# Second attention of a four-layer kernel: the masked sum cut to the masked keys, the open keys read by ScalarE, and a new table of places

## What is computed

```python
x = L0(x, ctx)                 # instance norm, attention over channels, 1x1 convolutions
x = L1(x, ctx, mask1)          # grouped attention, 32 heads on 8 key heads, residual, layer norm
# L2: queries from x, keys and values from ctx and x together (64 + 64 keys)
h    = concatenate([ctx, x], axis=1)
attn = einsum('bkhd,bnhd->bhkn', q(x), k(h)) / 16
full = concatenate([mask2.astype(bool), ones((b, 64), bool)], axis=-1)
attn = softmax(where(full[:, None, None, :], attn, -inf))
x    = mlp(rmsnorm(out(attn @ v(h)) + x)) + x
# L3: layer norm, token shift, five mixes, r k v g and a decay w
s_t  = k_t * v_t + w_t * s_(t-1);  out_t = r_t . (u * k_t * v_t + s_(t-1))
x    = x + (groupnorm(out) * gn_w + gn_b) * g @ Wo.T ; then a channel mix
```

## Time and profile before

| | us |
|---|---|
| median of 3 runs | 2051.25 (2050.09 to 2053.39) |
| the profiled execution | 2052.37 |
| its span, first to last instruction | 2050.3 |
| mean granted TensorE clock, of full | 0.931 |
| busy: TensorE, VectorE, ScalarE, GpSimd | 1742.5, 1383.6, 855.7, 818.8 |
| one group beside a layer 3 | 238.5 |

### The profile page before, as it was taken

The page is one execution under the profiler, slowest core; times in us unless marked ns, Lnnn a source line. Parts: engine busy times, 40 slices in busy tenths (PEclk is TensorE's granted clock), DMA queues, the critical chain, the costliest instruction groups (busy, mean ns, idle before and its releaser), DMA issues.

```text
span 2050.3 us, 36747 instructions
## 1 busy us (share of the span) xinstructions
PE 1742.5 (85%) x13613; PEld 1076.0 (52%) x13613; DVE 1383.6 (67%) x2332; ACT 855.7 (42%) x1687; POOL 818.8 (40%) x895
## 2 busy tenths in 40 slices
PE   3788898898988898898988989888988889888865
PEld 2565555564564645555555645646455555555213
DVE  3653579756886569946787567865788557983383
ACT  1445443444534434454534445344344444343202
POOL 3532147503664136702465036641366114760070
PEclk9999999999999999999989989999999999999757
DMA  6001011110211002110111102110021100210030
GB/s 171 1 1 34 1 22 42 23 43 1 46 25 42 18 1 59 28 26 18 27 38 23 43 1 43 28 43 17 1 59 28 27 17 17 48 23 12 0 83 11
DMA packets 73584, 60.92 MB, mean 30 GB/s; under 512 B 38960, under 2 KB 56512, under 8 KB 73408
## 3 DMA queue, kind: packets, MB, share of 16 engines
q1 hardware_dynamic: 49600, 41.70, 9.6%
q10 hardware_dynamic: 23264, 16.85, 3.0%
q0 software_dynamic: 544, 0.03, 0.0%
HBM read 20.28 MB, written 4.19 MB: 12 GB/s over the span
## 4 chain that ended last, share of the span: by engine, by line
PE 52%; DVE 19%; ACT 11%; issue 9%; POOL 6%; DVEq 0%; ACTq 0%; DMA 0%; POOLq 0%; SPq 0%
PE bank L639 24%; PE bank L974 5%; PE bank L776 5%; PE bank L655 3%; DVE seg_max L1415 3%; PE bank L871 3%; DVE late L1249 3%; DVE soft_ring L1409 3%; PE bank L716 2%; DVE late L1261 2%; POOL late L1537 2%; ACT soft_ring L1111 2%; POOL soft_ring L1575 2%; ACT soft_ring L1121 1%; PE bank L847 1%
## 5 line engine op out<-in xcount | busy, mean ns | idle before, releaser
L1575 POOL TENSOR_TENSOR soft_ring<-soft_ring,seg_max 128x512 f32<-128x512 f32 x256 | 286.0, 1130 | 343.7 <-DVE seg_max L1415 343.1
L1583 POOL TENSOR_SCALAR soft_ring<-soft_ring,rden 128x256 f32<-128x256 f32 x64 | 59.2, 925 | 511.0 <-DVE rden L1374 511.0
L1121 ACT ACTIVATE soft_ring<-soft_ring 128x512 f32<-128x512 f32 x256 | 160.3, 629 | 239.0 <-POOL soft_ring L1575 225.9
L1537 POOL TENSOR_TENSOR late<-late 128x520 f32<-128x520 f32 x128 | 198.2, 1549 | 124.8 <-DMA late<-late 64.8
L1249 DVE TENSOR_TENSOR_SCAN late<-late 128x520 f32<-128x520 f32 x128 | 218.7, 1709 | 15.3 <-DVE early L1430 4.4
L716 PE MATMUL bank<-late,pick 128*128 128x512 f32 x256 | 168.7, 756 | 35.6 <-DVE late L1261 35.1
L1409 DVE SCALAR_TENSOR_TENSOR soft_ring<-bank,mask 128x512 f32<-128x512 f32 x256 | 164.3, 683 | 19.2 <-PE bank L776 8.2
L917 PE MATMUL bank<-ident,soft_ring 128*128 128x128 f32 x1024 | 164.4, 288 | 9.0 <-ACT soft_ring L1121 6.8
L1415 DVE TENSOR_REDUCE seg_max<-soft_ring 128x8 f32<-128x512 f32 (+1 forms) x256 | 166.5, 677 | 6.2 <-DVE early L1472 2.0
L917 PEld LDWEIGHTS bank<-ident,soft_ring 128*128 128x128 f32 x1024 | 117.4, 144 | 95.1 <-issue 66.5
L776 PE MATMUL bank<-early 64*128 64x512 f32 (+1 forms) x512 | 118.5, 564 | 50.3 <-ACTq L1114 47.7
(11 more groups left out here) (240 smaller groups left out, 3337.6 us busy)
## 6 DMA issues: line engine op xcount, KB each, us to landing
late<-late SPq DMA_DIRECT2D x128, 260.0 KB, 3.0
c<-in_ctx ACTq DMA_DIRECT2D x8, 512.0 KB, 4.2
x<-in_x ACTq DMA_DIRECT2D x8, 512.0 KB, 5.3
out_x<-late SPq DMA_DIRECT2D x8, 512.0 KB, 2.9
mask<-in_mask_Bx1xSxS_ff ACTq DMA_DIRECT2D x16, 128.0 KB, 4.5
w<-in_L_xattn_mlp_w ACTq DMA_DIRECT2D x2, 1024.0 KB
mask<-in_mask_BxS_ik SPq DMA_DIRECT2D x8, 256.0 KB, 3.7
wkv<-in_L_xattn_kv_w ACTq DMA_DIRECT2D x1, 512.0 KB
```

The source lines that it names most:

```text
L1121: af(soft[:, u % SOFT, :], soft[:, u % SOFT, :], ACT.Exp).then_inc(sig("exp"), 1)
L1537: tt(aj[:, n % 2, :], kP[:, k, :, :].rearrange("p b t -> p (b t)"), vj[:, n % 3, :], ALU.mult).then_inc(sig("kv_done"), 1)
L1575: tt(s, s, seg_max[:, u % SOFT, 0:segs].unsqueeze(2).broadcast_to([128, segs, 512 // segs]), ALU.subtract).then_inc(sig("sub"), 1)
```

## The change

In the second attention `masked` covers only the first 64 keys of each of the four heads (128 x 256 in place of 128 x 512) and signals `masked2`. A new function on ScalarE, `open_keys`, waits for that signal, reads the other 64 keys of each head from the same bank, scales them and writes them to the same slot, and signals `open2`. It is called for both units of a pair in even iterations, behind `turned`. `largest` waits for both signals, and the bank is given back to TensorE there, by VectorE, and no longer by `masked`. `mask2` loses its half of zeros (and its memset, 128 x 1024, in the setup). The gate of layer 3 is written as two instructions with three operands in place of three (times, times-plus, times). And the tables `PLACES` and `SCAN_PLACES` have other numbers throughout: which step of the main loop a stage of layer 3 stands at, on each engine. The diff, without the counts of the semaphores, the memset and the mask's shapes:

```diff
@@ -509,41 +508,41 @@
 PACE = {"r u k": 2.2, "shift": 2.2, "maa": 2.2, "gate": 2.4, "shift 2": 2.2,
         "mix 4": 1.0, "r": 1.0, "v": 1.0, "decay": 1.0, "td": 1.2}
 PLACES = {
-    "moments": (0, 2, 0, 6),
-    "normalize": (11, 2, 6, 6),
-    "turn": (11, 11, 10, 6),
-    "shift": (11, 26, 15, 6),
-    "maa": (21, 27, 16, 6),
-    "mix 0": (25, 32, 25, 8),
-    "mix 1": (29, 32, 27, 16),
-    "td": (30, 32, 30, 17),
-    "k": (30, 32, 30, 19),
-    "mix 2": (30, 32, 31, 21),
-    "decay": (33, 32, 31, 21),
-    "v": (37, 34, 35, 21),
-    "mix 3": (37, 40, 36, 27),
-    "mix 4": (43, 40, 40, 32),
-    "r": (45, 43, 41, 43),
-    "g": (45, 44, 43, 43),
-    "r u k": (45, 45, 46, 53),
-    "bonus": (50, 52, 55, 55),
-    "center": (123, 123, 123, 127),
-    "variance": (123, 123, 123, 133),
-    "gate": (123, 123, 123, 133),
-    "project": (127, 127, 126, 133),
-    "moments 2": (130, 128, 126, 133),
-    "normalize 2": (130, 129, 132, 133),
-    "turn 2": (132, 130, 133, 133),
-    "shift 2": (133, 130, 133, 133),
-    "ffn k": (134, 133, 133, 133),
-    "ffn r": (134, 133, 133, 133),
-    "ffn v": (134, 133, 134, 133),
+    "moments": (1, 0, 0, 0),
+    "normalize": (1, 1, 1, 4),
+    "turn": (6, 3, 5, 4),
+    "shift": (10, 13, 6, 5),
+    "maa": (11, 21, 8, 5),
+    "mix 0": (25, 25, 24, 5),
+    "mix 1": (28, 27, 26, 5),
+    "td": (28, 28, 27, 5),
+    "k": (30, 30, 29, 18),
+    "mix 2": (33, 30, 33, 26),
+    "decay": (37, 34, 35, 26),
+    "v": (37, 34, 37, 39),
+    "mix 3": (37, 39, 37, 42),
+    "mix 4": (41, 43, 41, 42),
+    "r": (45, 43, 46, 45),
+    "g": (48, 47, 48, 48),
+    "r u k": (50, 66, 49, 48),
+    "bonus": (51, 76, 49, 48),
+    "center": (125, 124, 126, 128),
+    "variance": (127, 126, 126, 128),
+    "gate": (127, 128, 126, 128),
+    "project": (130, 128, 128, 128),
+    "moments 2": (130, 130, 128, 128),
+    "normalize 2": (131, 132, 131, 128),
+    "turn 2": (133, 132, 132, 128),
+    "shift 2": (134, 132, 133, 128),
+    "ffn k": (134, 133, 134, 131),
+    "ffn r": (134, 133, 134, 134),
+    "ffn v": (134, 133, 134, 137),
 }
 SCAN_PLACES = (
-    (50, 52, 64, 56), (50, 61, 65, 64), (61, 62, 68, 64), (69, 68, 69, 65), (70, 75, 70, 66),
-    (72, 81, 70, 66), (80, 85, 85, 70), (82, 100, 85, 82), (86, 100, 89, 94), (92, 107, 98, 102),
-    (103, 111, 105, 105), (103, 112, 107, 105), (110, 112, 107, 106), (110, 112, 107, 106), (111, 112, 109, 117),
-    (111, 112, 112, 117), (121, 123, 117, 123), (121, 123, 120, 123), (123, 123, 122, 126),
+    (62, 76, 57, 52), (63, 77, 64, 58), (67, 77, 67, 63), (67, 77, 68, 64), (70, 81, 68, 64),
+    (72, 81, 70, 70), (82, 81, 84, 71), (83, 86, 85, 84), (87, 89, 86, 86), (88, 89, 97, 94),
+    (94, 92, 100, 102), (107, 112, 106, 102), (109, 112, 107, 107), (111, 112, 109, 110), (115, 112, 112, 116),
+    (120, 113, 119, 128), (123, 113, 119, 128), (125, 117, 119, 128), (125, 118, 122, 128),
 )
 due = {}
 for stage in STAGES:
...
             if now:
                 sp.wait_ge(sig("max"), past("max"))
-            sp.dma_start(mask2[:, :, 0:L].bitcast(I32), mask2_in[now].unsqueeze(0).broadcast_to([128, NB, L])).then_inc(sig("mask2_in"), 16)
+            sp.dma_start(mask2[:, :, :].bitcast(I32), mask2_in[now].unsqueeze(0).broadcast_to([128, NB, L])).then_inc(sig("mask2_in"), 16)
...
@@ -1119,6 +1118,12 @@
             tables(LOG_EXP, TANH)
             act.wait_ge(sig("sub"), past("sub") + u + 1)
             af(soft[:, u % SOFT, :], soft[:, u % SOFT, :], ACT.Exp).then_inc(sig("exp"), 1)
+
+        def open_keys(u):
+            t, _ = take(act, ("s", u))
+            act.wait_ge(sig("masked2"), past("masked2") + u - UNITS + 1)
+            af(soft[:, u % SOFT, :].rearrange("p (h s) -> p h s", h=4)[:, :, L:KEYS], t[:, :].rearrange("p (h s) -> p h s", h=4)[:, :, L:KEYS],
+               ACT.Identity, scale=1.0 / HD2).then_inc(sig("open2"), 1)
 
         def turned(u):
             t, free = take(act, ("t", u))
@@ -1174,6 +1179,9 @@
             step()
             if unit(i - 3) >= 0:
                 turned(unit(i - 3))
+            if unit(i) >= UNITS and unit(i) % 2 == 0:
+                open_keys(unit(i))
+                open_keys(unit(i) + 1)
             if i < U0:
                 exps0(i)
             if 1 <= i < U0 + 1:
@@ -1311,9 +1319,9 @@
                 for k in range(KT):
                     dve.wait_ge(sig("oc_ready"), past("oc_ready") + k + 1)
                     dve.wait_ge(sig("rgn_ready"), past("rgn_ready") + k + 1)
-                    link(tt(ogT[:, k, :], ogT[:, k, :], rgn[:, k, :], ALU.mult))
-                    link(ts(ogT[:, k, :], ogT[:, k, :], v("gn_w", k), v("gn_b", k), ALU.mult, ALU.add))
-                    tt(ogT[:, k, :], ogT[:, k, :], gg[:, k, :], ALU.mult).then_inc(sig("ogT_ready"), 1)
+                    link(stt(out=ogT[:, k, :], in0=ogT[:, k, :], scalar=v("gn_w", k), in1=rgn[:, k, :], op0=ALU.mult, op1=ALU.mult))
+                    stt(out=ogT[:, k, :], in0=ogT[:, k, :], scalar=v("gn_b", k), in1=gg[:, k, :],
+                        op0=ALU.add, op1=ALU.mult).then_inc(sig("ogT_ready"), 1)
             elif stage == "project":
                 for q in range(2):
                     t, free = take(dve, (stage, q))
@@ -1405,13 +1413,23 @@
                 dve.wait_ge(sig("mask1_in"), past("mask1_in"))
             if u == UNITS:
                 dve.wait_ge(sig("mask2_ready"), past("mask2_ready") + 1)
-            mask, segs, n = (mask1[:, 2 * (u // 4) + u % 2, :], KVH, L) if u < UNITS else (mask2[:, (u - UNITS) // 2, :], 4, KEYS)
-            stt(out=cuts(u, soft[:, u % SOFT, :]), in0=cuts(u, t[:, :]), scalar=HD1 ** -0.5 if u < UNITS else 1.0 / HD2,
-                in1=mask.unsqueeze(1).broadcast_to([128, segs, n]), op0=ALU.mult, op1=ALU.add).then_inc(free, 1)
+            if u >= UNITS:
+                mask = mask2[:, (u - UNITS) // 2, :].unsqueeze(1).broadcast_to([128, 4, L])
+                stt(out=cuts(u, soft[:, u % SOFT, :])[:, :, 0:L], in0=cuts(u, t[:, :])[:, :, 0:L], scalar=1.0 / HD2, in1=mask,
+                    op0=ALU.mult, op1=ALU.add).then_inc(sig("masked2"), 1)
+                return
+            mask = mask1[:, 2 * (u // 4) + u % 2, :].unsqueeze(1).broadcast_to([128, KVH, L])
+            stt(out=cuts(u, soft[:, u % SOFT, :]), in0=cuts(u, t[:, :]), scalar=HD1 ** -0.5, in1=mask,
+                op0=ALU.mult, op1=ALU.add).then_inc(free, 1)
 
         def largest(u):
             b, k = spot(("s", u))
-            dve.wait_ge(sig(f"bank{b}_free"), k)
+            if u >= UNITS:
+                dve.wait_ge(sig("masked2"), past("masked2") + u - UNITS + 1)
+                dve.wait_ge(sig("open2"), past("open2") + u - UNITS + 1)
+                dve.sem_inc(sig(f"bank{b}_free"), 1)
+            else:
+                dve.wait_ge(sig(f"bank{b}_free"), k)
             nc.vector.tensor_reduce(seg_max[:, u % SOFT, 0:KVH if u < UNITS else 4], cuts(u, soft[:, u % SOFT, :]),
                                     X, ALU.max).then_inc(sig("max"), 1)
```

More of the change, by code:

```diff
@@ L154, in build @@
         mask1 = sb("mask1", [128, NB, L])
-        mask2 = sb("mask2", [128, NB, KEYS])
+        mask2 = sb("mask2", [128, NB, L])
         s0 = sb("s0", [128, KT, NB, HS])
@@ L311, in _ @@
                 nc.gpsimd.memset(eps5[:, :], 1e-5)
-                nc.gpsimd.memset(eps6[:, :], 1e-6)
                 nc.gpsimd.memset(ones32[:, 0:16], 1.0)
@@ L315, in _ @@
                 nc.gpsimd.memset(ones32[:, 32:48], 1.0)
-                link(nc.gpsimd.memset(mask2[:, :, :], 0.0))
+                link(nc.gpsimd.memset(eps6[:, :], 1e-6))
                 pool.sem_inc(sig("zeroed"), 1)
@@ L556, in build @@
             ahead_ready=8, at_ready=8, c0_in=16, cT_ready=2, edge_ready=1, exp=32, exp0=8, gT_ready=8, k2_ready=4, kT1_ready=1,
-            kbd_ready=4, lT_ready=4, mask1_in=32, mask2_in=16, mask2_ready=1, max=32, ml_ready=2, mm_ready=2, mn_ready=2,
-            mo_ready=4, nmax0_ready=8, over_ready=8, p0_ready=8, p0b_ready=8, pT0_ready=8, pT_ready=32, q1_ready=2, qring_ready=8,
-            rden0_ready=8, rstd0_ready=1, rstd1_ready=2, rstd2_ready=2, stats0_ready=1, stats1_ready=2, sub=32, v2_ready=4,
-            v2_zero=1, x0_in=16, x1T_ready=2, x1_ready=4, x3_ready=2, x_added=8, xh1_ready=4, xh2_ready=4, xnT_ready=4,
+            kbd_ready=4, lT_ready=4, mask1_in=32, mask2_in=16, mask2_ready=1, masked2=16, max=32, ml_ready=2, mm_ready=2,
+            mn_ready=2, mo_ready=4, nmax0_ready=8, open2=16, over_ready=8, p0_ready=8, p0b_ready=8, pT0_ready=8, pT_ready=32,
+            q1_ready=2, qring_ready=8, rden0_ready=8, rstd0_ready=1, rstd1_ready=2, rstd2_ready=2, stats0_ready=1, stats1_ready=2,
+            sub=32, v2_ready=4, v2_zero=1, x0_in=16, x1T_ready=2, x1_ready=4, x_added=8, xh1_ready=4, xh2_ready=4, xnT_ready=4,
             xr3_ready=4, xr_ready=8)
@@ L1605, in gpsimd_program @@
                         pool.wait_ge(sig("mask2_in"), past("mask2_in") + 16)
-                        m = mask2[:, :, 0:L]
```

(1 more changed line is left out.)

## The result

The changed kernel takes **2059.9 us** (median) against 2051.2 of the kernel before: ratio 1.0042, 95% interval 1.0029 to 1.0056. It is slower by 0.4%, and outside the range of 1985 to 2055. The profiled execution took 2061.03 (span 2059.0), 8.7 more than before's.

The account below looks back on a forecast made before the run. Neither TensorE (85% busy) nor VectorE (67%) was an outright bound; layer 0 and attention 2 with its tail offered time. Seven groups at -4.6 (-32.2), the first 0, memset -0.9, gate -1.1: -34.2, so 2017 us, range 1985 to 2055.

Parts of the forecast that it names:

- Half sums and open reads: Attention 2: VectorE's half sums at 0.41 and ScalarE's reads at 0.38, 4.3 us a group off VectorE.
- rival 4: Attention 2: ScalarE's open reads take 1.24 instead of 0.38, +13.8 a group, about 2115 us; chance 1%.
- Sum: +3.0: Attention 2: VectorE's new waits for ScalarE over a group's eight pairs, +3.0 us, bounds 0.5 and 14.4.
- the ring: Attention 2: maximum, GpSimd's subtraction, ScalarE's exponential, copy and open read, then the next pair's maximum; 4.0 us long.
- "0" for the first group: First group, without layer 3: gain and waits even out, 0 us, bounds -3 and +6.
- VectorE's saving counted at its full value: Attention 2: the 4.3 us saved on VectorE bring the last maximum earlier in full; net +2.3 with waits and scan.
- Scan 105 to 100, +3.6: Attention 2: layer 3's scan of step 105, moved to step 100 ahead of the last units, adds 3.6 us.
- Layer 0, -2.5: Layer 0: the turn and "maa" move into TensorE's gaps, saving 2.5 us a group, bounds 0 and -5.
- Tail, -6.9 and -0.8: Behind attention 2: -6.9 us from last maximum to last division, -0.8 from there to the MLP's first product.
- MLP, +2.8: MLP: "variance" costs its full 2.2 us there, plus about 0.6 for a flip that waits.
- two table loads more; they hide: MLP: ScalarE's two more table loads cost nothing, as it is busy 9.1 of 19.4 us.
- Rival 1: Attention 2: the waits decide and make it slower, 2088 us at 1.5 a pair; chance 14%, from 2055 up.

Follow-up runs that it names:

- e1: The split sum, open reads and new waits alone, with the places and gate of the kernel before: 2085.6 us, ratio 1.0168 against the kernel before.
- e3: The changed kernel, but ScalarE gives the bank back itself with its open read: 2055.7 us, ratio 1.0022 against the kernel before.
- e4: The changed kernel, but ScalarE issues both open reads ahead of the copy of unit u-3: 2046.6 us, ratio 0.9975 against the kernel before.
- e10: e4 with the next pair's masked query between second half sum and first maximum in six middle pairs: 2045.5 us, ratio 0.9962 against the kernel before.
- e2: The new places and two-instruction gate alone, with the masked sum of the kernel before: 2045.7 us, ratio 0.9968 against the kernel before.
- e8: e2 with the stages from "center" on, and the last three picks, put back: 2045.5 us, ratio 0.9966 against the kernel before.
- e7: e2 with the stages from "moments" to "g" at their places of before: 2056.6 us, ratio 1.0018 against the kernel before.

## Why the prediction was wrong, step by step

The forecast was -4.6 a group and 0 in the first; measured are +0.6 and +6.0.

- **Half sums and open reads: right.** 413 ns against 0.41, 381 ns against 0.38, 4.3 us a group of VectorE's time (64 pairs x 0.54 / 8). The rule of the Trainium skill (ScalarE: Activation LUTs, § Rules for kernel authors) that simple arithmetic belongs on VectorE, for which it gives a bf16 figure, isn't borne out for this fp32 shape out of a bank; rival 4 fell. As the Trainium skill (SBUF — State Buffer, § Who interferes with whom) implies, a half sum with one SBUF input doesn't feel GpSimd: 405 to 425 ns over all 128, with the same median (0.41 us) for the 70 that have no GpSimd instruction beside them and for the others.
- **"Sum: +3.0", the ring's waits: the first step that failed.** Measured 5.7. The ring had the right length (4.28 against 4.0), and pairs without other work did wait. By pair, mean of the seven groups: the second waits 0.92 (forecast 1.1), the third 0.42 (0.4), the fourth, with GpSimd's four products in front, 2.24 (1.5), the sixth 0.86 and the other four 0.28 each. So the three pairs that I named came to 3.6 instead of 3.0. What failed most is "the rest next to nothing", which came to 2.0: I asked only whether ScalarE would be late, and priced a pair in which it isn't at zero. Yet the round trip is there in every pair. Two rows of a pair with ScalarE free, VectorE's and ScalarE's, from 867.7 us:

```profile
867.73 0.76 DVE L1418 SCALAR_TENSOR_TENSOR soft_ring<-bank,mask 128x256 f32<-128x256 f32 x2 [0.31 <-DVE early L1448]
868.76 1.28 DVE L1433 TENSOR_REDUCE seg_max<-soft_ring 128x4 f32<-128x512 f32 x2 [0.28 <-ACT soft_ring L1125]
```
```profile
868.25 0.72 ACT L1125 ACTIVATE soft_ring<-bank 128x256 f32<-128x256 f32 x2 [1.60 <-DVE soft_ring L1418]
```

  The first half sum ends at 868.15, the read starts 0.10 later, runs 0.38, and the maximum starts 0.13 after it: 0.61, of which the second half sum covers 0.33. So 0.28 stays in each pair, 2.2 of the 5.7. My 0.05 for a signal was too little too: 0.13 passes from the end of the read to the start of the maximum.
- **"0" for the first group: failed.** It has no layer 3, so the whole ring lies open: a pair takes 4.88 (161.69 to 166.57). There VectorE is busy 27.0 of attention 2's 44.2 us (30.3 of 40.0 before). +6.0, at the bound that I had given; e1 shows +5.0 with the places unchanged. Only 4.2 of the 6.0 lie in attention 2. Another 1.7 lie in attention 1, whose program in this group is the same: it takes 46.8 or 48.5 there, from one run to the next, and the first group of the six kernels with the old sum and query takes 174.2 to 179.7. With the halved sum and the query where it was it takes 179.4 to 181.4, in six kernels. The bank held until the second maximum is not the reason: with ScalarE giving it back (e3), attention 2 of this group still takes 44.0, and with the open reads first (e4) 43.8. Only work between sum and maximum takes the loss away (e10: 39.4, and 176.6 for the group). Which link of the ring holds it in e4 stays open.
- **VectorE's saving counted at its full value: failed.** In attention 2 VectorE was busy 41.8 of 46.7, and I took the last maximum to come earlier by every microsecond saved. In the changed kernel that isn't what costs, as the waits there exceed the saving (5.6 less 4.3, and attention 2 takes 1.8 more than in e2). But had the waits been my 3.0, the gain wouldn't have come: in e10, 11 us of balance give 2 at most. VectorE stands idle 8.6 us of its attention 2, against 4.3 in e2, so what it saved, it waited. Part of that is the fourth pair (2.1), part the scores from TensorE; which of them sets the end was not isolated.
- **Scan 105 to 100, +3.6: too high.** Attention 2 grows by 2.3 in e2, but its price shows elsewhere too: TensorE's output projection waits for divisions that now stand behind scans (39 us, above).
- **Layer 0, -2.5, and end of attention 1, +0.5: failed.** I kept 2.5 of the 3.72 that "maa" fills. Layer 0 shrinks by 3.6, but TensorE's idle time in it is 8.0 against 7.5: the work went to attention 1, and the gaps stayed. The one of 3.31 is now

```profile
471.81 1.97 PE L775 MATMUL bank<-early 64*128 64x256 f32 x8 [4.13 <-ACTq L1113]
```

  since it ends with ScalarE's release, which the turn made later, not with TensorE's work. Over the three stretches I had -2.0 and the table has -0.1 (e2 +0.4). My test "layer 0 under 51.5" came true and proved nothing: a stretch is shorter also when its work has left.
- **Tail, -6.9 and -0.8: right.** 30.7 to 23.5, -7.2. **MLP, +2.8: too low**, +3.9. "variance" costs its two products (1.9), and gaps open in a stretch that had none (TensorE idle 3.0 against 0.6):

```profile
662.89 3.72 PE L654 MATMUL bank<-t_Wo,late 128*128 128x256 f32 x16 [0.98 <-DVE late L1323]
...
672.68 1.09 PE L646 MATMUL bank<-ident,late 128*128 128x128 f32 x8 [0.92 <-DVE late L1238]
```

  What failed here is "two table loads more; they hide". There are three more, and one stands between the two instructions that make the deviation for the normalization in front of that flip, in all seven groups. ScalarE's rows, then VectorE's:

```profile
669.39 0.30 ACT L994 ACTIVATE rstd<-mv,eps 128x4 f32<-128x4 f32 x1 [3.00 <-DVEq L1234]
669.71 1.28 ACT L995 ACT_TABLE_LOAD   x1
671.00 0.21 ACT L995 ACTIVATE rstd<-rstd 128x4 f32<-128x4 f32 x1
```
```profile
671.24 1.38 DVE L1238 TENSOR_SCALAR late<-late,mv,rstd 128x256 f32<-128x256 f32 x4 [1.94 <-ACT rstd L995]
```

  By my estimate from these rows, without the load of 1.28 the flip could start before TensorE's products end at 671.76, and the gap of 0.92 would close. Before, and in e8, no load stands there (63 loads in all) and the flip has no gap. That ScalarE was busy 9.1 of 19.4 us said nothing about where a load falls. e8 also shows that this move is an exchange and no gain: 28.4 and 43.2 against 23.5 and 47.6.
- **Memset -0.9 and gate -1.1:** the first group starts at 40.2 instead of 41.2 (40.2 to 41.4 in all the kernels, so this shows little), and the last block is 0.5 shorter.

Together: 7 x 0.6 + 6.0 - 1.5 = +8.7, as in the spans. Against -4.6, a group lost 1.9 from layer 0 to the stretch between, 1.1 in the MLP, 1.8 in attention 2, and 0.5 in the tail. Rival 1 came nearest, and I gave it too small a chance: its turning point, 7.6 us of waits, wasn't even reached. The kernel turned slower at 5.7 because the gains that I had set against them in layer 0 and in the MLP weren't there.

What stays open: why the front and the state stages pay only together. The square shows that it is so; which wait joins them was not isolated. None of these kernels is clearly faster than e2, e8 or e10, all 0.3 to 0.4% under before.

## What to carry over

When a step of an in-order engine is split so that its second half comes from another engine, price the round trip in every repetition, also where the other engine is free, and put independent work into it; here it took back more than the split saved. Count a saving on an engine up to the point where the next resource takes over, and a loss in full. Ask of ScalarE's table loads not whether they fit in its idle share but which instruction waits behind each. Read neighbouring stretches together: one that gets shorter may only have handed its work to the next, and idle time is what tells the two apart.

## What the runs showed of the hardware

- A round trip from VectorE to ScalarE and back takes 0.23 us besides the work in it (0.10 out, 0.13 back), at the end of attention 2 above; the 0.13 is the same in all 64 pairs, the 0.10 holds where ScalarE is free; around a read of 0.38 that is more than half as much again.
- TensorE's same 256 picks cost less after, in the same number of instructions (before, then after):

```profile
L716 PE MATMUL bank<-late,pick 128*128 128x512 f32 x256 | 168.7, 756 | 35.6 <-DVE late L1261 35.1
```
```profile
L715 PE MATMUL bank<-late,pick 128*128 128x512 f32 x256 | 153.3, 690 | 17.5 <-DVE late L1269 17.5
```

  15 of TensorE's 20 us. In e1, with the places of before, they take 168.8, in e2 152.3. The granted clock is 0.948 on average after and 0.931 before; in the tail, where many picks stand, it is 0.96 against 0.90 on the mean of the seven groups (0.89 to 0.94 before, 0.95 to 0.98 after). It is 0.947 in e2 and 0.928 in e1, so it goes with the places. In e2 TensorE is idle 11 us more than before, yet the span is 7.5 shorter: its whole gain comes as shorter matmuls. That the places cause the clock is what the four runs agree with; no run held the order and changed the clock alone. Within the executions of one kernel it moves too (0.939 to 0.948 in e7).
